# A ViT tower step on one core: mask block sums by TensorE, lo parts by GpSimd, a split first attention and a new prologue order

## The chip, the cores and the metric

One core of a Trainium2 chip runs the whole kernel. The metric is device time in microseconds of one execution, lower is better: 529.68 before, the median of three runs (529.33 to 531.19).

## What is computed

The reference makes a table of time kernels from `log_dt` and `Lambda`, contracts it with `x`, and adds two layers, each behind a layer norm without weights. `mask` is 1024 x 1024 int32; a 32 x 32 block of the attention weight stays if the sum of its mask entries is over zero.

```
P    = dt_Lambda[..., None] * pos - P_max[..., None]
h    = einsum('chn,hnl->chl', Wc, exp(P)).real            # 16 x 128 x 1024
block_mask = mask.reshape(32, 32, 32, 32).sum(axis=(1, 3)) > 0
h    = h + layernorm(h) @ (weight * elem_mask).T
z    = layernorm(h)
h    = h + z @ W_base.T + b_base + sum_e sparsemax(z @ W_router.T + b_router)_e * (z @ A_e) @ B_e
```

## The kernel before

**Tiles and parts.** The 16 x 128 rows of `h` are cut into 16 tiles of 128 rows by 1024 columns. Every large product runs on float32r operands in two parts, hi (the rounded value) and lo (what is left), as three products hi*hi, hi*lo, lo*hi: `product`, L457. One k-chunk of 128 therefore has three matmuls of 512 columns for each of the two column halves, and `attention(t, k)` (L498) and `base(t, k)` (L489) have six. `base` also carries the experts' last product (`experts`, L494).

**The prologue** loads and prepares the weights while the first tiles are made.
- SP's queue loads log_dt, the constants, then by turns eight blocks of 128 rows of the mask and of the attention weight, then x(1), the eight blocks of W_base, lora_A, x(2) and b_router (L324 to L335). Behind them `k_rows(t)` (L316) turns a tile through DRAM into `h1`.
- For weight block j VectorE sums 1024 int32 mask entries to 32 per row (`mask_sums`, L1006), TensorE adds them over 32 rows with one small matmul (`block_sums`, L369), and VectorE masks the weight and takes its row sums (`wa_mask`, L1015). ScalarE centres blocks 0 to 3 (`wa_centre`, L628), GpSimd blocks 4 to 7 (L887). TensorE transposes the block in two halves of four 128 x 128 pieces into the two banks of `acc_b` (`wa_transposes`, L385); ScalarE writes the hi half (`wa_copies`, L634); the lo half is a subtraction from PSUM on VectorE (`wa_lows`, L1023), or, for blocks 1, 3 and 5 (`BY_POOL`), ScalarE copies the bank to SBUF (L637) and GpSimd subtracts there (L892).
- W_base goes the same way without a mask: `wb_half(i)` (L408), `wb_highs` (L643), `wb_lows` (L1029), sixteen halves, two in flight.
- The table of a tile: `phases` and `v_factors` on VectorE, `exponentials` and `sines` on ScalarE, `table_v` on VectorE, `table_b` on GpSimd for tiles 0 to 2 (L876 to L879), and `k_transposed` on TensorE (L439). `k_high` (ScalarE) and `k_low` (VectorE, L1121) make the operands of the attention, `k_turn` (VectorE, L1127) the rows for SP.
- GpSimd's `parameters(r)` (L814) is a chain of 24 small operations; VectorE's `reciprocal_of_norm(r)` (L1001) waits for its tenth link, and GpSimd's end of the chain for that reciprocal.
- The first attention, tile 0, runs in column halves with transpositions in between (`first_attention`, L465, order L546 to L560), the second whole (L566). `attention_residual` (VectorE, L1145) reads all of `acc_a` and gives the row sum for the mean; ScalarE's `h2_centre` and `h2_deviation` follow, and `h2_transposes` (L448), `lora_router` (L479, L481), VectorE's `gates` (L1157 to L1168, which end in `hw_sb`), `gated_transpose` (L487), base and experts. GpSimd's `add_bias` (L917, L920) subtracts the mean and adds b_base; VectorE's `result` (L1187) closes a tile.

**The order** is written out by hand for each engine: TensorE L527 to L591, ScalarE L737 to L802, GpSimd L895 to L912, VectorE L1220 to L1320. Then `steps` runs the loop of all later tiles. Engines wait for each other by semaphores alone, so an instruction that waits holds everything behind it on its engine.

Of the kernel before, what the change touches and what calls it, by code (L numbers as in the profile page):

```python
# [21 lines left out]
P = 128  # L22
# [14 lines left out]
K_ALL = K_COL + 9  # L37
# [6 lines left out]
DT_STEPS = 14  # L44
ROUNDS = (slice(0, 2 * HT), slice(2 * HT, H))
# [3 lines left out]
def constants():  # L49
# [10 lines left out]
        [np.full(NA, NA - 1), np.full(NB0, NA * (NB0 - 1)), np.full(NB1, NA * NB0 * (NB1 - 1))])  # L60
    top = row < N
# [8 lines left out]
def build_vit_tower(nc, x, log_dt, lam, w_attn, mask, w_base, b_base, w_router, b_router, lora_a, lora_b,  # L70
# [4 lines left out]
    with ExitStack() as ctx:  # L75
# [19 lines left out]
        mask_raw, wb_hi = sb_twice("mask_raw", [P, NWT, L], I32, "wb_hi", [P, NWT, KC, P])  # L95
# [31 lines left out]
        x2_hi, x2_lo = sb("x2_hi", [P, KC, P], FR), sb("x2_lo", [P, KC, P], FR)  # L127
        h1 = sb("h1", [P, L])
# [4 lines left out]
        st1, st2 = sb("st1", [P, 8]), sb("st2", [P, 2, 8])  # L133
        gate = sb("gate", [P, 2, E, E])
# [3 lines left out]
        mask_sum = sb("mask_sum", [P, NWT, L // 32])  # L138
# [20 lines left out]
        mask_summed, blk_ready = sem("mask_summed"), sem("blk_ready")  # L159
# [5 lines left out]
        wb_t, wb_high, wb_low = (sem(n) for n in ("wb_t", "wb_high", "wb_low"))  # L165
# [15 lines left out]
        mean_added = sem("mean_added")  # L181
# [17 lines left out]
        def block_bank(j):  # L199

            bank = acc_a[:, HALF:L] if j % 2 else acc_a[:, 0:HALF] if j < NWT // 2 else small
            return bank[:, 0:L // 32]

        BY_POOL = (1, 3, 5)
        CENTRE_LAST = 4
# [99 lines left out]
        def _(sp):  # L307
# [60 lines left out]
        def _(pe):  # L368
            def block_sums(j):  # L369

                pe.wait_ge(mask_summed, j + 1)
                if j >= 2:
                    pe.wait_ge(wa_masked, j - 1)
                pe.matmul(block_bank(j), kst[:, K_BLK:K_BLK + P], mask_sum[:, j, :],
                          start=True, stop=True).then_inc(blk_ready, 1)
# [32 lines left out]
            def wb_half(i):  # L408
                j = i // 2
                if i >= 2:  # L410
                    pe.wait_ge(wb_high, i - 1)
                    pe.wait_ge(wb_low, i - 1)
# [52 lines left out]
            def first_attention(n, chunks, beside=None):  # L465

                for k in chunks:
                    mm = product(acc_a, x2_hi[:, k, :], x2_lo[:, k, :], wa_hi, wa_lo, k, k == 0, k == KC - 1, (n,))
                    if n == 1 and k == KC - 1:  # L470
# [60 lines left out]
            x_transposes(0)  # L531
            block_sums(2)
            wa_transposes(1)
            block_sums(3)
            wa_transposes(2)
            block_sums(4)
            k_transposed(0)
            wa_transposes(3)
            block_sums(5)
            block_sums(6)  # L540
            block_sums(7)
            wa_transposes(4)
            x_transposes(1)
            wa_transposes(5)
            pe.wait_ge(kt_lo, 1)
            wa_rows_ready(NWT // 2)  # L546
            first_attention(0, range(0, 2))
            wa_transposes(6)
            first_attention(0, range(2, 4))
            wa_transposes(7)  # L550
            first_attention(0, range(4, 6))
            pe.wait_ge(rt_in, 16)
            pe.transpose(small[:, HALF - rt_rows:HALF], rt_stage, ident[0:rt_rows, 0:rt_rows]).then_inc(rt_t, 1)
            x_transposes(2)
            wb_half(0)
            wb_half(1)
            first_attention(0, range(6, KC))
            k_transposed(1)
            wa_rows_ready(NWT)
            first_attention(1, range(KC), {0: 2, 2: 3, 3: 4, 4: 5, 6: 6, 7: 7})  # L560
            wb_half(8)

            pe.wait_ge(h2_ready, 1)
            pe.wait_ge(kt_lo, 2)
            half = {1: 9, 2: 10, 3: 11, 4: 12, 5: 13, 6: 14}
            for k in range(KC):  # L566
                attention(1, k)
                if k == KC // 2 - 1:
                    pe.wait_ge(kt_turned, 2)
                    h2_transposes(0, 0)  # L570
                if k in half:
                    wb_half(half[k])
            wb_half(15)
# [5 lines left out]
            for k in range(KC):  # L579
                if k == KC // 2:  # L580
                    k_transposed(2)
                if k == KC - 3:
                    x_transposes(3)
                if k == KC - 2:
                    gated_transpose(0)
                base(0, k)
# [24 lines left out]
        def _(act):  # L611
            def q_tanh(r):
# [26 lines left out]
            def wb_highs(i):  # L639
                act.wait_ge(wb_t, i + 1)  # L640
                if i == 0:
                    act.wait_ge(mask_summed, NWT)
                act.activation(half_of(wb_hi, i), half_bank(i), ACT.Copy).then_inc(wb_high, 1)  # L643

# [30 lines left out]
            def k_high(t):  # L675

                act.wait_ge(kt_ready, t + 1)
                if later(t, 2):
                    act.wait_ge(attn_ready, t)
                act.activation(by_pair(x1_of(t)[0]), kt_pairs, ACT.Copy).then_inc(kt_hi, 1)  # L680

            def h2_centre(t, par):
# [5 lines left out]
                act.activation(h2[par][:, :], h2[par][:, :], ACT.Identity, bias=s[:, 1:2]).then_inc(h2_centred, 1)  # L688

# [54 lines left out]
            act.wait_ge(consts_in, 16)  # L744
            wa_centre(0)
            x_rows_twice(0)
# [3 lines left out]
            sines(0)  # L750
            wa_copies(0)
            sines(1)
            q_sines(1)
            wa_centre(1)
            wa_copies(1)
            wa_centre(2)
            wa_copies(2)
            wa_centre(3)
            x_rows_twice(1)
            q_tanh(1)  # L760
            exponentials(1)
            k_high(0)
            wa_copies(3)
            wa_copies(4)
            wa_copies(5)
            wa_copies(6)
            x_rows_twice(2)
            wa_copies(7)
            wb_highs(0)
            wb_highs(1)  # L770
            k_high(1)
            for i in range(2, 6):
                wb_highs(i)
            k_sum(0)
            k_deviation(0)
            wb_highs(6)
            wb_highs(7)
            act.wait_ge(lora_in, 16 * KC)
            act.wait_ge(rt_copied, 1)
            act.activation(wr[:, :, 0, :], cat_raw, ACT.Copy).then_inc(cat_hi, 1)  # L780
            wb_highs(8)
            exponentials(2)
            h2_centre(0, 0)
            wb_highs(9)
            wb_highs(10)
            sines(2)
            wb_highs(11)
            wb_highs(12)
            h2_high(0)
            for i in range(13, 2 * NWT):  # L790
                wb_highs(i)
            k_sum(1)
            k_deviation(1)
            h2_deviation(0, 0)
            act.wait_ge(lorb_in, 16)
            act.activation(lb_hi[:, :], lb_raw[:, :], ACT.Copy).then_inc(lorb_hi, 1)
            x_rows_twice(3)
            exp_and_sin(3)
            k_high(2)
            gated_high(0)  # L800
            h2_centre(1, 1)
# [4 lines left out]
            act.wait_ge(attn_ready, TILES)  # L806
# [6 lines left out]
        def _(pool):  # L813
            def parameters(r):  # L814
# [79 lines left out]

            parameters(0)  # L895
# [6 lines left out]
            wa_centre(7)  # L902
# [433 lines left out]
```

## Time and profile before

| | |
|---|---|
| median of 3 runs | 529.68 us |
| span of the profiled execution, first to last instruction | 527.4 us |
| time of the profiled execution around its span | not shown |
| TensorE busy | 482.6 us (91% of the span) |
| VectorE, ScalarE, GpSimd busy | 410.9, 256.1, 125.7 us |
| mean granted TensorE clock | 0.982 of full speed |
| VectorE in the first tenth of the span | 70 to 90% or more |
| TensorE from 114.57 us to 500 us | busy 385.43 of 385.43 us |

How to read it: the shares of the whole span say that TensorE bounds the run, but they are an average over two stages. The loop, from 114.57 us on, has TensorE busy all the time. The prologue has it idle or at the lower clock for a good part, and there other engines and the loads set the pace. Matmul ends are modelled, so a busy stretch can hold matmuls at either clock level; the duration of a known piece of work tells which.

### The profile page before, as it was taken

How to read it: one execution, taken by the hardware profiler on the slowest of the kernel's cores; microseconds unless marked ns; L12 is line 12 of the kernel's file. 1: busy time of each engine (PE TensorE's matmuls, PEld its weight loads, DVE VectorE, ACT ScalarE, POOL GpSimd, SP SyncE). 2: the span in 40 equal slices, each digit the busy share in tenths (PEclk: the TensorE clock that was granted, in tenths of full speed). 3: DMA queues.
4: the chain of work that ended last, by engine and by line, in shares of the span. 5: the costliest groups of instructions: out<-in, count | busy, mean ns of one | idle time of the engine just before them, and what ended most of it. 6: DMA issues, size and time to landing. Idle time of an engine off the chain costs nothing.

```text
span 527.4 us, 7434 instructions
## 1 busy us (share of the span) xinstructions
PE 482.6 (91%) x2467; PEld 408.0 (77%) x2467; DVE 410.9 (78%) x866; ACT 256.1 (49%) x469; POOL 125.7 (24%) x110
## 2 busy tenths in 40 slices
PE   2256978979999999999999999999999999999995
PEld 2155757868888888888888888888888888888884
DVE  7989966898888988888888888888878888864241
ACT  3763385956463644546464636363645546223200
POOL 0577952631020303030303020110303030303020
PEclk9996989989999999999999999999999999999999
DMA  8995013022212112120304030212121120303011
GB/s 288 402 312 104 2 41 125 1 57 73 80 47 80 45 48 77 40 85 10 114 0 116 9 93 31 82 42 80 45 70 57 40 81 20 101 15 107 1 40 40
DMA packets 28763, 40.82 MB, mean 77 GB/s; under 512 B 10760, under 2 KB 21192, under 8 KB 28744
## 3 DMA queue, kind: packets, MB, share of 16 engines
q1 hardware_dynamic: 28368, 40.49, 25.3%
q8 instruction: 10, 0.16, 0.1%
q10 hardware_dynamic: 376, 0.10, 0.1%
q14 instruction: 9, 0.07, 0.0%
HBM read 23.80 MB, written 16.78 MB: 77 GB/s over the span
## 4 chain that ended last, share of the span: by engine, by line
PE 86%; DVE 6%; issue 2%; ACT 2%; DMA 1%; POOL 1%; SPq 0%; DVEq 0%; POOLq 0%
PE acc_b L455 36%; PE acc_a L455 33%; PE turnp L439 5%; PE small L479 4%; PE turnp L448 3%; PE small L481 1%; DMA mask_raw<-in_L_attn_mask 1%; PE acc_b L420 1%; DVE wa_raw L1015 1%; PE acc_b L399 1%; DVE mask_sum L1006 1%; PE xps L429 1%; DVE wa_lo L1023 0%; ACT L710 0%; ACT junk L708 0%
## 5 line engine op out<-in xcount | busy, mean ns | idle before, releaser
L917 POOL TENSOR_TENSOR h<-h,st 128x1024 f32<-128x1024 f32 x16 | 30.3, 1895 | 331.0 <-PE turnp L448 331.0
L455 PE MATMUL acc_a<-wa_hi,x_hi 128*128 128x512 f32 x256 | 84.3, 405 | 0.5 <-DVE h L1145 0.5
L455 PE MATMUL acc_b<-wb_hi,x_hi 128*128 128x512 f32 x256 | 84.6, 407 | 0.0
L455 PE MATMUL acc_a<-wa_lo,x_hi 128*128 128x512 f32 x256 | 81.6, 395 | 0.0
L455 PE MATMUL acc_b<-wb_lo,x_hi 128*128 128x512 f32 x256 | 81.3, 394 | 0.0
L455 PE MATMUL acc_a<-wa_hi,x_lo 128*128 128x512 f32 x256 | 81.3, 394 | 0.0
L455 PE MATMUL acc_b<-wb_hi,x_lo 128*128 128x512 f32 x256 | 80.9, 392 | 0.0
L455 PEld LDWEIGHTS acc_a<-wa_hi,x_lo 128*128 128x128 f32 x256 | 48.7, 190 | 10.5
L455 PEld LDWEIGHTS acc_a<-wa_lo,x_hi 128*128 128x128 f32 x256 | 48.9, 191 | 10.2
L455 PEld LDWEIGHTS acc_b<-wb_lo,x_hi 128*128 128x128 f32 x256 | 48.5, 190 | 10.5
L455 PEld LDWEIGHTS acc_b<-wb_hi,x_lo 128*128 128x128 f32 x256 | 48.5, 189 | 10.6
L715 ACT ACTIVATE x_hi<-turnp 128x1024 fp32r<-128x1024 f32 x16 | 16.4, 1025 | 81.0 <-PE turnp L448 81.0
L455 PEld LDWEIGHTS acc_a<-wa_hi,x_hi 128*128 128x128 f32 x256 | 47.1, 191 | 9.1 <-DVE h L1145 0.8
L455 PEld LDWEIGHTS acc_b<-wb_hi,x_hi 128*128 128x128 f32 x256 | 45.0, 190 | 8.2
L1187 DVE SCALAR_TENSOR_TENSOR h<-acc_b,st,h 128x1024 f32<-128x1024 f32 (+1 forms) x17 | 20.7, 1220 | 25.6 <-PE acc_b L455 25.6
L920 POOL TENSOR_TENSOR h<-h,bias 128x1024 f32<-128x1024 f32 x16 | 39.3, 2455 | 1.3
L1121 DVE TENSOR_TENSOR x_lo<-turnp,x_hi 128x1024 fp32r<-128x1024 f32 x16 | 19.6, 1223 | 21.9 <-ACT x_hi L680 21.9
L439 PEld LDWEIGHTS turnp<-v_sb,b_sb 128*128 128x128 f32 x256 | 32.6, 200 | 5.2 <-issue 4.0
L439 PE MATMUL turnp<-v_sb,b_sb 128*128 128x128 f32 x256 | 32.9, 284 | 3.9 <-POOL b_sb L879 3.9
L721 ACT ACTIVATE hw_hi<-small 128x128 fp32r<-128x128 f32 x16 | 4.4, 278 | 60.4 <-PE small L487 60.4
L479 PE MATMUL small<-wr,x_hi 128*128 128x272 f32 x128 | 32.2, 338 | 0.0
L655 ACT ACTIVATE er_t<-er_t 128x256 f32<-128x256 f32 x15 | 6.3, 418 | 49.7 <-DVE er_t L1044 49.7
(201 smaller groups left out, 936.5 us busy)
## 6 DMA issues: line engine op xcount, KB each, us to landing
h<-rows_out SPq DMA_DIRECT2D x16, 512.0 KB, 3.2
out<-h SPq DMA_DIRECT2D x15, 512.0 KB
rows_out<-b_sb SPq DMA_DIRECT2D x56, 128.0 KB, 2.3
mask_raw<-in_L_attn_mask SPq DMA_DIRECT2D x8, 512.0 KB, 9.6
wa_raw<-in_L_attn_weight SPq DMA_DIRECT2D x8, 512.0 KB, 10.2
wb_raw<-in_L_ffn_W_base SPq DMA_DIRECT2D x8, 512.0 KB, 14.9
rows_out<-tmp SPq DMA_DIRECT2D x8, 128.0 KB, 2.3
xn<-in_x SPq DMA_DIRECT2D x15, 64.0 KB
```

The lines of the kernel that those rows point to most:

```text
L399: mm = pe.transpose(half_bank(i)[:, k * P:(k + 1) * P], every_eighth, ident)
L420: mm = pe.transpose(half_bank(i)[:, k * P:(k + 1) * P], wb_rows[j][:, c:c + P], ident)
L439: mm = pe.matmul(kt_pairs[:, h // HG, :, h % HG * C:(h % HG + 1) * C], b_sb[:, h, :, :].rearrange("p x y -> p (x y)"), v_sb[:, h, :, :], s ...
L448: mm = pe.transpose(turnp[:, k * P:(k + 1) * P], h2[par][:, k * P:(k + 1) * P], ident)
L455: return pe.matmul(cols, a, rows, start=first, stop=last)
L479: pe.matmul(small[:, 0:2 * CAT], x_hi[:, k, :], wr[:, k, :, :].rearrange("p s n -> p (s n)"), start=k == 0, stop=False)
L655: act.activation(er_of(t), er_of(t), ACT.Exp).then_inc(tab_exp, 1)
L715: act.activation(x2_of(t)[0][:, :, :].rearrange("p k n -> p (k n)"), turnp[:, :], ACT.Copy)\
L917: pool.tensor_tensor(h2[par][:, :], h2[par][:, :], st2[:, par, 1:2].to_broadcast([P, L]), ALU.subtract)\
L920: pool.tensor_tensor(h2[par][:, :], h2[par][:, :], bias[:, :], ALU.add).then_inc(bias_added, 1)
L1121: dve.tensor_tensor(by_pair(lo), kt_pairs, by_pair(hi).bitcast(F), ALU.subtract).then_inc(kt_lo, 1)
L1187: dve.scalar_tensor_tensor(h, acc_b[:, cols], st2[:, par, 4:5], h, ALU.mult, ALU.add).then_inc(out_ready, 1)
```

## The change

- The mask is turned into numbers in place: blocks 0 to 3 by GpSimd, first in its queue, blocks 4 to 7 by ScalarE. TensorE then sums it over rows with a matrix of ones and zeros (`pick`, placed so that block j adds into rows 4j to 4j + 3), in three groups (0, 1), (2, 3), (4 to 7); VectorE reduces each group's 32 x 1024 sums to 32 x 32; TensorE spreads them over the rows with a second matrix (`spread`, in the place of `h1`).
- Blocks 1 and 4 of W_base get their lo parts from GpSimd: ScalarE copies the transposed bank to SBUF (`wb_copies`), GpSimd subtracts.
- The attentions of tiles 0 and 1 both run by column halves. The first residual is taken by halves too, and the mean is put together from two sums (`first_centre`).
- The last operation of `reciprocal_deviation` is a tensor_scalar in place of a tensor_tensor. SP's `k_rows(0)` waits for all block sums, GpSimd's first `add_bias` for `hw_ready`.
- The order of the prologue is another one on all four engines. The loop of the later tiles is not touched beyond that one operation and the count of `attn_ready`, which starts with tile 1.

The diff's core:

```diff
+MASK_GROUPS = ((0, 1), (2, 3), (4, 5, 6, 7))
+    k[:, K_PICK:K_PICK + PICK] = np.arange(PICK)[None, :] == L // 32 - 4 + row[:, None] // 32
...
+        WB_BY_POOL = (1, 4)
...
             def k_rows(t):
                 sp.wait_ge(kt_turned, t + 1)
+                if at(t, 0):
+                    sp.wait_ge(blk_ready, NWT)
...
-            def block_sums(j):
-                pe.wait_ge(mask_summed, j + 1)
-                if j >= 2:
-                    pe.wait_ge(wa_masked, j - 1)
-                pe.matmul(block_bank(j), kst[:, K_BLK:K_BLK + P], mask_sum[:, j, :],
-                          start=True, stop=True).then_inc(blk_ready, 1)
+            def mask_by_rows(j):
+                g = GROUP_OF[j]
+                first, last = j == MASK_GROUPS[g][0], j == MASK_GROUPS[g][-1]
+                if j == 0:
+                    pe.wait_ge(pick_ready, 1)
+                if g >= 2 and first:
+                    pe.wait_ge(mask_summed, g - 1)
+                pe.wait_ge(mask_cast[j], 1)
+                for n in range(2):
+                    mm = pe.matmul(rows_bank(g)[:, n * HALF:(n + 1) * HALF], pick[:, MB - 4 - 4 * j:2 * MB - 4 - 4 * j],
+                                   mask_num[:, j, n * HALF:(n + 1) * HALF], start=first, stop=last)
+                if last:
+                    mm.then_inc(mask_rowed, 1)
+            def block_sums(g):
+                if g == 0:
+                    pe.wait_ge(spread_ready, 1)
+                    pe.wait_ge(turn_step, 3)
+                else:
+                    pe.wait_ge(wa_masked, MASK_GROUPS[g][0])
+                pe.wait_ge(mask_summed, g + 1)
+                for j in MASK_GROUPS[g]:
+                    mm = pe.matmul(block_bank(j), spread[:, j * P:(j + 1) * P], mask_sum[:, g, :], start=True, stop=True)
+                mm.then_inc(blk_ready, len(MASK_GROUPS[g]))
...
+            mask_by_rows(0)
             dt_transposes()
+            mask_by_rows(1)
+            mask_by_rows(2)
+            mask_by_rows(3)
             block_sums(0)
             block_sums(1)
+            x_transposes(0)
             wa_transposes(0)
+            mask_by_rows(4)
+            mask_by_rows(5)
+            mask_by_rows(6)
+            mask_by_rows(7)
+            wa_transposes(1)
+            wa_transposes(2)
             block_sums(2)
             k_transposed(0)
             wa_transposes(3)
+            x_transposes(1)
             wa_transposes(4)
...
             wa_transposes(5)
+            wa_transposes(6)
+            wa_transposes(7)
...
+            attention_half(0, 0, (4,))
             wb_half(0)
             wb_half(1)
+            attention_half(0, 0, (5,))
...
+            wb_half(2)
+            wb_half(3)
             k_transposed(1)
+            wb_half(4)
+            wb_half(5)
...
+            pe.wait_ge(h2_half, 1)
+            pe.wait_ge(kt_lo, 2)
+            attention_half(1, 0, (0,))
...
+            pe.wait_ge(kt_turned, 2)
+            h2_transposes(0, 0)
...
+            pe.wait_ge(h2_ready, 1)
+            attention_half(1, 1, (0,))
...
             lora_router(0)
+            wb_half(14)
+            wb_half(15)
+            k_transposed(2)
             pe.wait_ge(wb_high, 2 * NWT)
-            pe.wait_ge(wb_low, 2 * NWT)
+            pe.wait_ge(wb_low, len(wb_direct))
+            pe.wait_ge(wb_low_pool, len(WB_BY_POOL))
...
+            def mask_numbers(j):
+                act.wait_ge(mask_in[j], 16)
+                act.activation(mask_num[:, j, :], mask_rows[j], ACT.Copy).then_inc(mask_cast[j], 1)
...
+            def wb_copies(i):
+                act.wait_ge(wb_t, i // 2 * 2 + 2)
+                act.activation(wb_raw[:, i // 2, i % 2 * HALF:(i % 2 + 1) * HALF], half_bank(i), ACT.Copy)\
+                    .then_inc(wb_copied, 1)
...
+            def first_centre():
+                s = st2[:, 0, :]
+                act.wait_ge(h2_half, 1)
+                act.activation(half_mean[:, 0:1], s[:, 0:1], ACT.Copy, scale=-1.0 / L).then_inc(h2_mean_half, 1)
+                act.wait_ge(h2_ready, 1)
...
+            mask_numbers(4)
+            x_rows_twice(0)
+            wa_centre(0)
+            wa_centre(1)
+            mask_numbers(5)
+            mask_numbers(6)
+            sines(1)
+            mask_numbers(7)
             wa_copies(0)
...
+            wb_highs(3)
+            wb_copies(2)
+            wb_copies(3)
+            k_high(1)
+            exponentials(2)
...
+            sines(2)
+            first_centre()
+            wb_highs(6)
+            h2_deviation(0, 0)
...
+            mask_numbers(0)
+            mask_numbers(1)
+            mask_numbers(2)
+            mask_numbers(3)
             parameters(0)
             table_b(0)
...
             table_b(2)
+            wb_lows(1)
+            wb_lows(4)
             pool.wait_ge(lorb_hi, 1)
...
             pool.wait_ge(bias_in, 16)
+            pool.wait_ge(hw_ready, 1)
             add_bias(0, 0)
...
-            def mask_sums(j):
-                dve.wait_ge(mask_in[j], 16)
-                dve.tensor_reduce(mask_sum[:, j, :], mask_rows[j].rearrange("p (k b) -> p k b", b=32), AX.X, ALU.add)\
+            def mask_sums(g):
+                dve.wait_ge(mask_rowed, g + 1)
+                dve.tensor_reduce(mask_sum[:, g, :], rows_bank(g).rearrange("p (k b) -> p k b", b=32), AX.X, ALU.add)\
                     .then_inc(mask_summed, 1)
...
-                dve.tensor_tensor(s[:, 4:5], s[:, 5:6], s[:, 7:8], ALU.mult).then_inc(s_chain, 1)
+                dve.tensor_scalar(s[:, 4:5], s[:, 5:6], s[:, 7:8], None, ALU.mult).then_inc(s_chain, 1)
```

VectorE's order up to the first result is now: dt_exponential, signs, dec_and_turn, phases(0), mask_sums(0), q_arguments(0) and (1), reciprocal_of_tanh(0), mask_sums(1), wa_mask(0) and (1), reciprocal_of_norm(0), decay_b(0), phases(1), v_factors(0), wa_mask(2) and (3), wa_lows(0), mask_sums(2), table_v(0), wa_mask(4), wa_lows(2), wa_mask(5) to (7), wa_lows(4), decay_b(1), k_low(0), k_turn(0), the router's copy, wa_lows(6), v_factors(1), wa_lows(7), reciprocal_of_tanh(1), wb_lows(0) and (1), table_v(1), phases(2), k_low(1), h1_reciprocal(0), first_residual(0) and (1), reciprocal_of_norm(1), k_turn(1), wb_lows(4) and (5), decay_b(2), v_factors(2), phases(3), wb_lows(6) and (7), table_v(2), wb_lows(10) and (11), h2_low(0), wb_lows(12) to (15), h2_reciprocal(0), gates(0), h1_reciprocal(1), attention_residual(1), gated_low(0), k_low(2), k_turn(2), v_factors(3), table_v(3), result(0).

## Rows read from the trace of the kernel before

**Rows 1.** Windows: us, busy time and instructions by engine, clock, DMA, GB/s

```profile
0.00:48.57 48.57, 18.78 (x87) 17.05 (x87) 42.41 (x96) 24.89 (x52) 23.18 (x43) 0.92 0.87 289
48.57:114.57 66.00, 56.86 (x295) 45.89 (x294) 52.25 (x98) 43.61 (x77) 37.29 (x37) 0.93 0.13 43
114.57:500.00 385.43, 385.43 (x1988) 327.38 (x1987) 308.47 (x651) 186.09 (x338) 60.98 (x28) 1.00 0.21 59
```

**Rows 2.** Timeline of TensorE, 46 to 110: start, length, instruction, [idle before, releaser]

```profile
46.97 1.95 PE L399 MATMUL acc_b<-kst,wa_raw 128*128 128x128 f32 x8 [3.16 <-DVE wa_lo L1023]
...
53.82 1.28 PE L399 MATMUL acc_b<-kst,wa_raw 128*128 128x128 f32 x8
...
65.32 0.63 PE L420 MATMUL acc_b<-kst,wb_raw 128*128 128x128 f32 x4 [0.55 <-ACT wb_hi L643]
...
71.09 0.63 PE L420 MATMUL acc_b<-kst,wb_raw 128*128 128x128 f32 x4 [1.49 <-issue]
73.53 0.63 PE L420 MATMUL acc_b<-kst,wb_raw 128*128 128x128 f32 x4 [1.81 <-ACT wb_hi L643]
...
90.90 0.63 PE L420 MATMUL acc_b<-kst,wb_raw 128*128 128x128 f32 x4 [0.97 <-issue]
...
108.71 0.33 PE L487 MATMUL small<-kst,hw_sb 128*128 128x128 f32 x1 [3.19 <-DVE hw_sb L1168]
```

**Rows 3.** Chain of waits, 55 to 133: start, length, engine, tile, line, count

```profile
55.10 1.40 PE acc_a L455 x6
...
74.69 4.61 PE acc_a L455 x12
...
82.94 0.87 PE turnp L448 x8
...
85.65 0.44 PE acc_b L420 x4
...
109.04 5.69 PE acc_b L455 x18
...
115.60 10.93 PE acc_a L455 x48
126.53 1.79 PE turnp L439 x16
...
130.17 2.82 PE acc_b L455 x12
```

**Rows 4.** Timeline of VectorE: columns as in rows 2

```profile
38.57 1.23 DVE L1015 SCALAR_TENSOR_TENSOR wa_raw<-acc_a,wa_raw 128x1024 f32<-128x1024 f32 x1 [2.24 <-PE acc_a L374]
...
46.13 0.09 DVE L1015 DVE_READ_ACCUMULATOR wa_raw<-acc_a,wa_raw 128x1 f32 x1
...
56.45 1.81 DVE L995 TENSOR_SCALAR lb_raw<-bias 128x224 f32<-128x224 f32 x1
...
101.13 1.79 DVE L1139 TENSOR_TENSOR st<-st 128x1 f32<-128x1 f32 x1
```

**Rows 5.** Groups by line and shape, 0 to 115: busy, mean ns, idle before

```profile
L1006 DVE TENSOR_REDUCE mask_sum<-mask_raw 128x32 f32<-128x1024 int32 x8 | 9.6, 1212 | 0.2
...
L892 POOL TENSOR_TENSOR wa_lo<-wa_raw,wa_hi 128x1024 fp32r<-128x1024 f32 x3 | 7.1, 2378 | 0.0
...
L1023 DVE TENSOR_TENSOR wa_lo<-acc_b,wa_hi 128x512 fp32r<-128x512 f32 x10 | 6.4, 682 | 1.0 <-ACT wa_hi L634 1.0
...
L887 POOL TENSOR_SCALAR wa_raw<-wa_raw,wa_neg 128x1024 f32<-128x1024 f32 x4 | 4.5, 1120 | 0.4
L1127 DVE STREAM_TRANSPOSE tmp<-turnp 128x1024 f32<-128x1024 f32 x2 | 4.1, 2072 | 0.0
```

**Rows 6.** Tile view of mask_raw, window 5.4:5.8 (block 3, issued at 5.44)

```profile
DMA to landing us min/median/max: 9.1/9.1/9.1
```

**Rows 7.** Timeline of GpSimd: columns as in rows 2

```profile
55.73 2.39 POOL L892 TENSOR_TENSOR wa_lo<-wa_raw,wa_hi 128x1024 fp32r<-128x1024 f32 x1
...
100.54 2.37 POOL L912 TENSOR_TENSOR lb_lo<-lb_raw,lb_hi 128x1024 fp32r<-128x1024 f32 x1 [3.94 <-ACT lb_hi L796]
```

More of the change, by code:

```diff
@@ L127, in build_vit_tower @@
         x2_hi, x2_lo = sb("x2_hi", [P, KC, P], FR), sb("x2_lo", [P, KC, P], FR)
+        with nc.sbuf_tensor("spread", [L // 32, L], F) as spread:
+            pass
         h1 = sb("h1", [P, L])
@@ L199, in block_bank, with rows_bank @@
         def block_bank(j):
[L201 to L202 removed]
+            return small[:, j * MB:(j + 1) * MB]
+        def rows_bank(g):
+            return (turnp if g == 1 else acc_a)[0:MB, :]
         BY_POOL = (1, 3, 5)
+        WB_BY_POOL = (1, 4)
+        wb_direct = [i for i in range(2 * NWT) if i // 2 not in WB_BY_POOL]
+        wb_raws = [i for i in range(2 * NWT) if i // 2 in WB_BY_POOL]
         CENTRE_LAST = 4
@@ L544, in _ @@
             wa_transposes(5)
+            wa_transposes(6)
+            wa_transposes(7)
+            pe.wait_ge(mask_summed, len(MASK_GROUPS))
             pe.wait_ge(kt_lo, 1)
             wa_rows_ready(NWT // 2)
[L547 to L553, printed above, removed]
@@ L564, in _ @@
[L564 to L573, printed above, removed]
+            attention_half(0, 0, (5,))
+            attention_half(0, 0, (6,))
+            attention_half(0, 0, (7,))
@@ L574, in _ @@
+            wb_half(13)
             pe.wait_ge(h2t_lo, 1)
@@ L576, in _ @@
             lora_router(0)
+            wb_half(14)
+            wb_half(15)
+            k_transposed(2)
             pe.wait_ge(wb_high, 2 * NWT)
-            pe.wait_ge(wb_low, 2 * NWT)
[L579 to L586, printed above, removed]
+            pe.wait_ge(wb_low, len(wb_direct))
+            pe.wait_ge(wb_low_pool, len(WB_BY_POOL))
+            base(0, 0)
+            base(0, 1)
+            base(0, 2)
+            base(0, 3)
+            gated_transpose(0)
+            base(0, 4)
+            base(0, 5)
+            base(0, 6)
+            base(0, 7)
             pe.wait_ge(lorb_lo, 1)
@@ L1253, in _ @@
             decay_b(1)
-            v_factors(1)
-            table_v(1)
-            wa_lows(6)
-            wa_lows(7)
-            reciprocal_of_tanh(1)
+            k_low(0)
+            k_turn(0)
             dve.wait_ge(rt_t, 1)
@@ L1262, in _ @@
                             small[:, HALF - rt_rows:HALF].rearrange("p (e k) -> p k e", e=E)).then_inc(rt_copied, 1)
+            wa_lows(6)
+            v_factors(1)
+            wa_lows(7)
+            reciprocal_of_tanh(1)
             wb_lows(0)
             wb_lows(1)
+            table_v(1)
             phases(2)
-            for i in range(2, 5):
-                wb_lows(i)
             k_low(1)
+            h1_reciprocal(0)
+            first_residual(0)
+            dve.wait_ge(b_ready, 2)
+            first_residual(1)
+            reciprocal_of_norm(1)
             k_turn(1)
+            wb_lows(4)
             wb_lows(5)
-            h1_reciprocal(0)
-            wb_lows(6)
-            dve.wait_ge(b_ready, 2)
-            attention_residual(0, 0)
-            wb_lows(7)
-            wb_lows(8)
-            reciprocal_of_norm(1)
-            wb_lows(9)
-            wb_lows(10)
             decay_b(2)
             v_factors(2)
+            phases(3)
+            wb_lows(6)
+            wb_lows(7)
+            table_v(2)
+            wb_lows(10)
             wb_lows(11)
-            phases(3)
+            h2_low(0)
             wb_lows(12)
-            h2_low(0)
             wb_lows(13)
```

207 lines of the change are left out of this document (130 added, 77 removed).

## The prediction

> **What bounds the kernel now.** The stages by windows come first [rows 1]. From 114.57 us on TensorE is busy without a gap at the full granted clock, and the loop that runs there has the same instructions in the same order after the change. So I price only how early TensorE reaches that point, the end of the first FFN's experts. Between 48.57, the first attention matmul, and 114.57 it is busy 56.9 of 66.0 us, part of that at the low level.
>
> The TensorE timeline says where it stood [rows 2]: 0.55 and 1.81 for a ScalarE copy of a wb half, 1.49 before a wb half, 0.97 before another, 3.19 for `hw_sb`: 8.0 us in five places. The chain of waits shows what follows a long wait [rows 3]: 48 attention matmuls take 10.93, so 12 should take 2.73 and 18 should take 4.10; after the waits at 74.69 and 109.04 they took 4.61 and 5.69. Clock thus cost 1.9 and 1.6.
>
> The same view prices the work: an attention 10.93, k_transposed 1.79, h2_transposes 0.87, a wb half 0.44, lora_router 130.17 - 128.32 = 1.85; base has 48 matmuls like an attention, experts six, 1.37. Two attentions, base, experts, sixteen wb halves, two k_transposed, one h2_transposes and one router make 47.5 us. At 55.10 all wa rows were transposed and four half chunks done (2.8 by the 1.40 of two), so a TensorE that never waits would have ended at 55.10 + 44.7 = 99.8. It ended at 114.57: 14.8 lost, of which 8.0 + 3.5 are named; 3.3 are short waits and small transposes, which I carry over whole.
>
> **Start: when the last wa rows are transposed.** Before, wa_transposes(7) ran at 53.82 [rows 2], and the masks that feed it were the end of VectorE's queue: wa_mask(7) ended at 46.2 [rows 4]. VectorE was full up to there, so its queue is the sum. Removed: eight mask reductions, 8 x 1.14 net of overlap (1.21 each) = 9.1, and k_low(0) and k_turn(0), now behind the masks, 1.2 (a pass, as a reduction) + 2.0 with overlap = 3.2 [rows 5]. Added: three reductions over 32 partitions, same length per partition, 3.6. Gone: the wait of 2.2 at 38.57 [rows 4].
>
> New waits: (a) dt_transposes stands on TensorE behind block 0's two matmuls; these wait for a GpSimd conversion. A 128x1024 one-input pass on GpSimd takes 1.12 and one with two inputs 2.38 [rows 5]; no row shows the int32 one. I take 1.12, the same inputs and shape, and keep 2.38. VectorE needs dt_transposes next, so it stands where it used to reduce block 0: 1.12 and 0.9 in front of them, 2.1 with the hand-over. (b) Block 3 lands 9.1 after its issue, at 14.5 [rows 6]; plus 1.12 and two matmuls of 512 columns (0.45 each, an estimate above the mean of 4.61 / 12 in a stretch partly at the low level) it is at 16.5, where VectorE would come at 15.6: 0.9 of waiting. (c) GpSimd starts `parameters(0)` behind four conversions, about 1.5 later, and VectorE's reciprocal_of_norm(0) with everything queued behind it waits that long. (d) wa_mask(4) waits for block_sums(2), which TensorE has behind wa_transposes(2): 0.8. (e) two-input VectorE work beside the conversions is held, below: 1.3. Sum 46.2 - 9.1 - 3.2 + 3.6 - 2.2 + 2.1 + 0.9 + 1.5 + 0.8 + 1.3 = 41.9.
>
> From there VectorE has two lo pairs, 1.25 each with overlap (0.68 a half) [rows 5], a decay (0.8, an estimate from pass lengths), k_low 1.2 and k_turn 2.1 before wa_transposes(7) is free: 41.9 + 6.6 = 48.5. It begins when the first half pair is done, 47.9, and eight cold transposes take 1.95 [rows 2]; I take 50.4 as its end. Ends: 48.5 with no holds, 55 with a 2.38 conversion and every hold.
>
> **What is held.** L1139, a two-input operation of one element per partition, took 1.79 from 101.13 and ended at 102.92, with the GpSimd subtraction that ran from 100.54 to 102.91 [rows 4, 7]. So two-input VectorE work waits for the GpSimd instruction in flight. Its replacement by a tensor_scalar stays off the path now. New on the path is table_v(2)'s last addition: both inputs in SBUF, and by my order it meets table_b(2) on GpSimd; 1.6, ends 0 and 2.4. [...]
>
> **Then TensorE's queue from 50.4.** 47.5 of work and 3.3 carried make 101.2. The first twelve matmuls come after scattered work and pay 1.9 [rows 3]. The big wait, for attention_residual(0), goes: column half 0 of attention(0) is read by first_residual(0) while half 1 runs. By my count TensorE wants it at about 68 and VectorE has it at 67.4, behind table_v(1), phases(2), k_low(1) and the reciprocals: cover half a us, and each us past it costs one. What is late next is h2_transposes(0), which needs both residuals and ScalarE's centring behind sines(2): 0.8, ends 0 and 4. The wait for `hw_sb` goes: h2_deviation(0) moves ahead in ScalarE's queue, and add_bias(0) waits for hw_ready, so the gates are not held; VectorE ends them at about 93, TensorE asks at 96. Behind that new wait GpSimd has only later biases, and result(0) stands behind table_v(3) on VectorE anyway.
>
> Four wb lo halves go to GpSimd: two passes of 2.38 plus four ScalarE copies in place of four VectorE ones of 0.68; GpSimd is otherwise free after table_b(2) and is done at about 88, base asks at 91. The wait put into SP's first k_rows holds k_rows(1), lora_B, bias and x loads, but its eight block sums are out by 37 and the turn it waits for anyway comes at 47. The four ScalarE conversions stand between loads; their end is in (d). The selectors, the sixteen mask matmuls and the block sums cost nothing by themselves: up to 48.57 TensorE is busy 18.8 us and ScalarE 24.9 [rows 1]. Were that cover gone, the matmuls would add 16 x 0.45 = 7.2.
>
> End 101.2 + 1.9 + 0.8 + 1.6 = 105.5 against 114.57: 9.1 saved. The profiled span is 527.4, so 518.3; what lies around a span is not shown, the median of the runs is 2.3 above it, so **520.5**.
>
> **Rivals.** [...] 0.12. *The wait is only moved*: VectorE or ScalarE brings the first residual or its centring as late as before, TensorE again stands about 4 and pays the clock 1.9, 5.5 beyond my 0.8: 526.0. For it: a cover of half a us. Against: the split, and VectorE has four lo halves, 2.7 us, less. 0.11. Both together: 529.2, no change, 0.06. *Slower: conversion on GpSimd*. If int32 to float costs far more there than any pass in the trace, four of them in a row set mask block 3: 5.4 + 4c in place of 15.6. The saving is gone at c = 4.8, and at c = 7 the kernel takes 538. For it: no integer row on GpSimd, which the kernel now starts with. Against: its 128x1024 passes lie between 1.1 and 2.5. 0.06.
>
> **How the numbers follow.** 0.65 for the forecast, whose own range is 514.5 (no holds, no cold start, no centring wait, 5.6 less, with 0.4 at the start) to 523. The range goes on to 526.5 for the first two rivals, 8 in 10. A change of 0.5%, 2.6 us, is about what can be told from none: faster 0.65 + 0.12 + 0.11 = 0.88, same 0.06, slower 0.06.
>
> **What would show it.** In the changed profile: conversions on GpSimd near 1.1 each; the last wa_mask ended by 42 and the last wa transposition by 50.4; no wait over 1 us of TensorE between the attentions; no wait for `hw_sb`; TensorE busy without gap from about 105 on, and the loop as long as before. Wrong would be conversions over 2.6, an hw_sb wait, or a wait of several us for the first residual.

## The result, and the profile after

The changed kernel takes 527.87 us, the median of ten runs (523.77 to 528.86), beside 530.68 for the kernel before in ten runs (529.20 to 531.58): a ratio of 0.9944, 95% interval 0.9922 to 0.9965. That is 2.8 us faster, where 9.1 were forecast, and 1.4 us above the upper end of the forecast range, 526.5. The profiled execution took 528.11, its span 526.3.

First the windows of the changed kernel, columns as in rows 1: up to the first attention matmul, and the window of the loop that rows 1 has for the kernel before.

```profile
0.00:52.88 52.88, 28.76 (x119) 21.35 (x120) 40.89 (x97) 32.79 (x64) 29.63 (x48) 0.83 0.79 263
...
114.57:500.00 385.43, 385.43 (x1953) 321.56 (x1952) 299.34 (x639) 181.64 (x329) 57.16 (x27) 1.00 0.20 56
```

Then its chain of waits, columns as in rows 3. L440 is a wa transposition, L499 a 512-column matmul, L492 h2_transposes.

```profile
46.90 1.17 ACT wa_hi L734 x2
48.07 0.50 ACT wa_raw L737
48.70 1.73 PE acc_b L440 x8
50.45 0.70 DVE wa_lo L1168
51.29 1.94 PE acc_b L440 x8
53.23 4.77 PE acc_a L499 x15
...
105.69 0.87 PE turnp L492 x8
106.56 11.20 PE acc_a L499 x48
...
121.40 2.84 PE acc_b L499 x12
...
135.24 11.20 PE acc_a L499 x48
```

Read it from the middle. h2_transposes(1), with which the loop begins, starts at 105.69; in the chain of before it starts 0.87 ahead of the attention at 115.60 [rows 3], at 114.73. The prologue is 9.04 us shorter. From there to the end of the span it takes 526.3 - 105.69 = 420.6, and before 527.4 - 114.73 = 412.7. **The loop is 7.9 us longer**, and that is where the gain went. 9.04 less 7.9 is the 1.1 by which the two spans differ; the medians differ by 2.8, as single executions of either kernel spread by more than 2.

It is longer without a wait and at the same granted clock: from 114.57 to 500 TensorE is busy 385.43 of 385.43 us at 1.00 in both, with 1953 matmuls on record instead of 1988 [rows 1]. What differs is the pace of the 512-column matmuls: 48 of them take 11.20, 233.3 ns each, where they took 10.93, 227.7 [rows 3]; 12 take 2.84, where they took 2.82. Transpositions keep their 0.87 [rows 3]. A tile goes from 106.56 to 135.24, 28.68 us, and in the chain of before from 115.60 [rows 3] to 143.77, 28.17:

```profile
143.77 10.92 PE acc_a L455 x48
```

### The profile page after: what moved, and what is told of

It is laid out like the page before. It is cut to its first block, busy times and chain, and to the rows that moved or that the text cites. A ratio compares the mean times of both kernels' runs of the same rounds, so it can differ in the third digit from the quotient of the medians.

```text
span 526.3 us, 7475 instructions
## 1 busy us (share of the span) xinstructions
PE 495.0 (94%) x2483; PEld 409.4 (78%) x2483; DVE 400.8 (76%) x859; ACT 261.9 (50%) x480; POOL 135.6 (26%) x116
## 4 chain that ended last, share of the span: by engine, by line
PE 90%; ACT 3%; DVE 3%; POOL 1%; issue 1%; DMA 1%; SPq 0%; DVEq 0%; ACTq 0%
PE acc_b L499 38%; PE acc_a L499 33%; PE turnp L483 6%; PE small L525 4%; PE turnp L492 3%; PE acc_b L440 2%; PE small L527 2%; PE acc_b L464 1%; DMA mask_raw<-in_L_attn_mask 1%; ACT wa_hi L734 1%; PE xps L473 1%; DVE wa_raw L1160 0%; PE small L415 0%; PE small L533 0%; ACT wa_raw L737 0%
## 5 line engine op out<-in xcount | busy, mean ns | idle before, releaser
L499 PE MATMUL acc_a<-wa_hi,x_hi 128*128 128x512 f32 x256 | 85.5, 405 | 0.0
L499 PE MATMUL acc_b<-wb_hi,x_hi 128*128 128x512 f32 x256 | 84.8, 407 | 0.0
L499 PE MATMUL acc_a<-wa_hi,x_lo 128*128 128x512 f32 x256 | 83.5, 397 | 0.0
L499 PE MATMUL acc_a<-wa_lo,x_hi 128*128 128x512 f32 x256 | 83.5, 397 | 0.0
L499 PE MATMUL acc_b<-wb_lo,x_hi 128*128 128x512 f32 x256 | 81.8, 396 | 0.0
L499 PE MATMUL acc_b<-wb_hi,x_lo 128*128 128x512 f32 x256 | 81.7, 395 | 0.0
L499 PEld LDWEIGHTS acc_a<-wa_hi,x_lo 128*128 128x128 f32 x256 | 48.4, 189 | 11.7
L499 PEld LDWEIGHTS acc_a<-wa_lo,x_hi 128*128 128x128 f32 x256 | 48.5, 190 | 11.4
L499 PEld LDWEIGHTS acc_b<-wb_hi,x_lo 128*128 128x128 f32 x256 | 48.1, 188 | 11.7
L499 PEld LDWEIGHTS acc_b<-wb_lo,x_hi 128*128 128x128 f32 x256 | 48.1, 188 | 11.4
L499 PEld LDWEIGHTS acc_a<-wa_hi,x_hi 128*128 128x128 f32 x256 | 47.5, 190 | 10.2
L499 PEld LDWEIGHTS acc_b<-wb_hi,x_hi 128*128 128x128 f32 x256 | 44.8, 189 | 9.1
L1272 DVE STREAM_TRANSPOSE b_sb<-turnp 128x1024 f32<-128x1024 f32 x14 | 31.3, 2239 | 0.0
```

The lines of the kernel that those rows point to most:

```text
L499: return pe.matmul(cols, a, rows, start=first, stop=last)
L1272: dve.transpose(turned_of(t).rearrange("p (g x a) -> p g a x", g=G, a=NA), kt_pairs).then_inc(kt_turned, 1)
```

## Experiments

TensorE's instructions in the loop are the same.
### The place of the tiles, moved in both kernels

Edits: to the changed kernel 32 bytes behind `kst` (e1), or in front of `x1_hi` (e3); to the kernel before 224 bytes behind `kst` (e2); e4 is the changed kernel once more.

```diff
         kst = sb("kst", [P, K_ALL])
+        sb("pad", [P, 8])
```

> The changed kernel with 32 unused bytes per partition behind the constants, so that every tile behind them begins at a multiple of 64 bytes again, as before the change; nothing else differs. Theory A (the loop got longer by where the operands of the products lie in SBUF): 48 attention matmuls of the loop take 10.92 again in place of 11.20, a tile's period 28.13 in place of 28.66, the span is 8 us shorter, about 518.3, and the time near 520. Rival B (the pace of the loop belongs to the execution: a fuller prologue, the chip or the activity): 11.20 stays, and the time stays at 527 to 528.

> The kernel before with 224 unused bytes per partition behind the constants, so that every tile behind them lies where the change puts it; order and instructions are those of before. Theory A: 48 attention matmuls of the loop take 11.20, the prologue's end stays near 114.6, and the time is 8 us longer, 537 to 539. Rival B: 10.92 stays and the time stays at 529 to 531.

> The changed kernel with the 32 unused bytes only in front of the hi and lo parts of h (x1_hi and all tiles behind it begin at a multiple of 64 bytes, the tables, v_sb and b_sb do not). If it is the operands of attention and base that count (theory A in its narrow form): 48 attention matmuls take 10.92 and the span is about 518 to 519. If tiles in front of them count as well: between 10.92 and 11.20. Rival B: 11.20 and a span of 526.

> The changed kernel once more, as it is. Theory A: 48 attention matmuls take 11.20 again and the prologue ends near 105.5, in every execution. Rival B in the form that the pace changes from one execution to the next: anything between 10.9 and 11.2.

The kernel after with 32 bytes took 519.48 (six runs, 517.85 to 522.48), a ratio to the kernel before of 0.9797 (0.9769 to 0.9824); the kernel before with 224 bytes took 538.74 (four runs), 1.0163 (1.0139 to 1.0187). e3 took 519.43 in one execution, e4 527.21. Chain of waits of e1:

```profile
106.28 0.87 PE turnp L493 x8
...
128.94 5.47 PE acc_b L500 x24
...
135.28 10.92 PE acc_a L500 x48
```

and of e2:

```profile
116.34 0.87 PE turnp L449 x8
...
145.87 11.21 PE acc_a L456 x48
```

Each kernel takes the other's pace with its place. The loops are 519.0 - 106.28 = 412.7 for e1 and 536.9 - 116.34 = 420.6 for e2; e3 gives 412.6, e4 420.5. So it is shown that the 7.9 us are a matter of placement and not of the prologue's new order, and e3 puts it on the x tiles or on what lies behind them.

### Which tiles, and which rule

Edits: e5 puts x1 and x2 where e1 has them and everything behind them 128 bytes beyond where the change had it, so that it stays off; e6 puts everything behind `kst` at 64 modulo 128; e7, on e1, moves `wa_hi`, a moving operand, by 32 bytes, and everything behind it, x1 and x2 too, by 128.

```diff
+        sb("pad", [P, 8])
         x1_hi = sb("x1_hi", [P, KC, P], FR)
...
         x2_hi, x2_lo = sb("x2_hi", [P, KC, P], FR), sb("x2_lo", [P, KC, P], FR)
+        sb("pad2", [P, 24])
```

> The kernel after, with 32 bytes in front of x1_hi and 96 bytes behind x2_lo: x1 and x2 (hi and lo) begin at multiples of 128 bytes again (193920 and on), and every tile behind them stays where the changed kernel had it, at 32 modulo 64. Theory (the stationary x tiles alone count): 48 attention matmuls take 10.9, and the time from the start of h2_transposes(1) to the end of the span is 412.7 plus at most 0.6, since the experts' stationary hw_hi and hw_lo stay off (6 of the 102 matmuls of 512 columns in a tile, 16 tiles, 6 ns each). Rival (a tile behind them counts, h1, h2 or hw): 11.2 and 420.5.

> The kernel after, with 96 bytes behind kst: x1_hi begins at 193984, which is 64 modulo 128. Theory (a start at a multiple of 64 is enough): 48 attention matmuls in 10.9, the loop 412.7. Rival (it must be a multiple of 128): 11.2 and 420.5, as with 96 modulo 128.

> The kernel after with the 32 bytes behind kst, and wa_hi alone, the moving operand of 32 of the 48 attention matmuls, 32 bytes off (114848, 32 modulo 64); everything else at the place modulo 128 that it had. Theory (only the stationary operand counts): 48 matmuls in 10.9, the loop 412.7. Rival (either operand counts): 10.92 + 32 x 0.006 = 11.11, and the loop 16 x 0.19 = 3.0 longer, 415.7.

They took 521.14, 529.38 and 527.87, one execution each. Chain of waits of e5 (the x24 are base and, at its end, the experts' six):

```profile
105.17 0.87 PE turnp L494 x8
...
127.88 5.55 PE acc_b L501 x24
...
134.31 10.93 PE acc_a L501 x48
```

of e6:

```profile
106.91 0.87 PE turnp L493 x8
...
136.47 11.20 PE acc_a L500 x48
```

and of e7:

```profile
106.33 0.88 PE turnp L495 x8
...
129.38 5.57 PE acc_b L502 x24
...
135.82 11.18 PE acc_a L502 x48
```

e5 says that the attention's pace is that of the x tiles: 10.93, with every tile behind them still off. Its loop is 1.4 longer than e1's, where at most 0.6 was expected: the group with the experts' six, whose stationary tiles stayed off, takes 5.55 against 5.47 in e1. e6 is slow, 420.7: a start at a multiple of 64 is not enough. e7 overturned the theory: with x at 0 modulo 256 the attention is slow, and so is the base product, whose own operands stayed at multiples of 128. Its 48 matmuls take 11.18, not the rival's 11.11, so "either operand's 32 bytes" does not fit either. What fits the attention and the base product in all of them is the distance: x1_hi lies a multiple of 256 bytes behind wa_hi in the kernel before, e1, e3 and e5, and 224, 224, 64 and 96 off in after, e2, e6 and e7; x2_hi lay 128 off wb_hi in e7.

### The distance of the two operands

Edits, both on e1: e12 moves all tiles by 32 bytes, so that the distances stay; e13 moves x1 and x2 alone by 128.

```diff
+        sb("pad2", [P, 8])
         wa_raw, wa_lo = sb_twice("wa_raw", [P, NWT, L], F, "wa_lo", [P, NWT, KC, P])
```

> The kernel after with the 32 bytes behind kst, and 32 bytes in front of the first tile, so that every tile, stationary or moving, begins 32 bytes further on and the distances between them stay (x1_hi 193952, wa_hi 114848, wa_lo 16544). Theory now (the distance between the stationary and the moving operand counts, and must be a multiple of 256 bytes; it fits the slow base product of the run with wa_hi moved, where x2 stood 128 off, and the slow run with x 64 off): 48 attention matmuls in 10.9, the loop 412.7. Rival (each operand's own address modulo 256 counts, 128 being the fast one): 11.2 and 420.5.

> The kernel after with the 32 bytes behind kst, and x1 and x2 (hi and lo) alone 128 bytes further on (194048); the tiles behind them 256 further. Theory (the distance must be a multiple of 256): 48 attention matmuls in 11.2, the loop 16 x 0.49 longer at 420, the experts' six matmuls alone at the old pace. Rival (a multiple of 128 is enough, and the run with wa_hi moved was slow from wa_hi's 32 bytes alone): 10.9 and 412.7.

They took 519.95 and 526.02, one execution each. Chain of waits of e12:

```profile
105.42 0.87 PE turnp L494 x8
...
134.43 10.92 PE acc_a L501 x48
```

and of e13:

```profile
104.52 0.87 PE turnp L495 x8
...
127.57 5.58 PE acc_b L502 x24
...
134.03 11.15 PE acc_a L502 x48
```

| run | x1_hi starts at | wa_hi starts at | distance modulo 256 | 48 matmuls | loop |
|---|---|---|---|---|---|
| before | 193664 | 114816 | 0 | 10.93 | 412.7 |
| after, e4, e2 | 193888 | 114816 | 224 | 11.19 to 11.21 | 420.5 to 420.6 |
| e1, e3 | 193920 | 114816 | 0 | 10.90 to 10.92 | 412.6 to 412.7 |
| e5 | 193920 | 114816 | 0 | 10.93 | 414.1 |
| e6 | 193984 | 114816 | 64 | 11.20 | 420.7 |
| e7 | 194048 | 114848 | 96 (128 to wa_lo) | 11.18 | 419.8 |
| e12 | 193952 | 114848 | 0 | 10.92 | 412.7 |
| e13 | 194048 | 114816 | 128 | 11.15 | 419.7 |

(Starts are bytes within a partition, in the compiled program.) In e12 wa, wb and x start 32 bytes off a multiple of 64, and the loop is as fast as before. In e13 they all start at multiples of 128, and it is slow. So in the attention and the base product the distance fits every run, and of those tried only multiples of 256 bytes are fast.

Two things keep this from being a rule. The experts' six matmuls do not follow it: in e13 their `hw` and `lb` lie a multiple of 256 bytes apart, at the places modulo 256 that they have in e1, and the old pace was expected of them, but base and experts together take 5.58, against 5.47 in e1. Read one by one from the traces, the experts' matmuls start 231 to 232 ns apart in e13, and in e7 too, where the distance is also a multiple of 256 (70 steps each); it is 226.6 in e1 and 233.4 in the changed kernel. Whether the pace of the base matmuls just before carries over or something else counts is open. And the distance is not separated from the start of x alone: x1 starts at 128 or 160 modulo 256 in all fast runs, at 0, 96 or 192 in all slow ones. A run with x at 160 and wa at 128 would tell, and there is none. Which matmul's moving operand it is, the one that streams while the next weights are loaded (weight loads are busy 321.56 of the 385.43 us of the changed kernel's window above, in which the matmuls leave no gap) or the matmul's own, these runs can't tell, since hi and lo of a weight lie a multiple of 256 apart (but for e7). Why it costs 5.8 ns a matmul stays open too.

### What the prologue's parts carry

All on e1. e8 and e14 take the first residual half only when both column halves are done, as the unsplit one did; e15 is e1 once more.

```diff
-                dve.wait_ge(attn_half, n + 1)
+                dve.wait_ge(attn_half, 2)
```

> The kernel after with the 32 bytes behind kst, and first_residual(0) waiting for both column halves of attention(0). From the end of wa_transposes(7) to the start of h2_transposes(1) the two profiles with the x tiles at 64 bytes took 51.9 and 52.0. Theory (the split hides one residual half, and what is lost is that half): TensorE waits about 1.0 (0.75 and the hand-over) for h2_half in front of attention(1), the centring comes 0.8 later too, and the stretch takes 53 to 53.5. Rival (the split is what kept the wait of several us and the clock away): 55 or more, with attention(1) at a lower granted clock.

> The kernel with first_residual(0) waiting for both column halves of attention(0) once more, timed in rounds beside the split one. Its single look, 516.3, had a higher granted clock in the wa transpositions (0.78 against 0.59 to 0.70 from 30 to 50), and from wa_transposes(7) on took 51.6 against 51.9. Theory (the early start was chance, the split hides only what ScalarE's queue in front of the centring would have hidden): median within 1 us of the split kernel's 519.5. Rival (the whole residual is better in itself): 516 to 517. Rival (the split is worth its half): 520.5 to 521.5.

> The kernel after with the 32 bytes behind kst once more, for comparison on the same chip: 519.5, as before, and 517.9 to 522.5 in single executions. If the granted clock of the start is what spreads them, a profile with a higher clock from 30 to 50 ends the prologue earlier by as much.

e8 took 516.29 in one execution; in four each, e14 took 519.57 (517.25 to 521.15, ratio 0.9788, 0.9746 to 0.9831) and e15 519.86 (519.53 to 521.40, ratio 0.9805, 0.9775 to 0.9835). **The split is worth nothing that can be told.** TensorE's waits from 52 to 106 in e14 (columns: what waited, for what, us in total, times, longest):

```profile
PE acc_a L500 <- DVE h L1300: 0.9, 1, 0.9
PE acc_b L465 <- issue: 0.2, 1, 0.2
```

and in e15, with the split:

```profile
PE turnp L493 <- ACT h L806: 1.1, 1, 1.1
```

Without the split TensorE waits 0.9 for the residual, and then no longer waits for the centring: the same wait, one step earlier. The wait of several us that the rival foresaw isn't there in either. e8's lead was made before: TensorE's timeline has, in e8,

```profile
29.89 1.28 PE L441 MATMUL acc_b<-kst,wa_raw 128*128 128x128 f32 x8 [0.71 <-DVE wa_lo L1169]
```

and in e1

```profile
30.39 1.94 PE L441 MATMUL acc_b<-kst,wa_raw 128*128 128x128 f32 x8 [0.59 <-DVE wa_lo L1169]
```

This is the same work at the high and at the low level: the granted clock is 1.00 in the 1.28 us and 0.50 in the 1.94. From 30 to 50 us it is 0.78 in e8 and 0.59 in e1. The last wa transposition then ends at 50.20 in e8, at 54.29 in e1. In e15 the clock of that stretch is 0.71, the end 53.01.

e9 gives the lo parts of wb blocks 1 and 4 back to VectorE, in the places of its queue where they stood before relative to `k_low(1)` and `table_v(2)`, and takes ScalarE's copies out.

```diff
-        WB_BY_POOL = (1, 4)
+        WB_BY_POOL = ()
...
+            wb_lows(2)
+            wb_lows(3)
             k_low(1)
...
+            wb_lows(8)
+            wb_lows(9)
             table_v(2)
```

> The kernel after with the 32 bytes behind kst, and the lo parts of wb blocks 1 and 4 by VectorE again, in front of k_low(1) and of table_v(2), without ScalarE's four copies. Theory (VectorE's queue feeds the first residual and the base product): two lo halves, 1.36, stand in front of the first residual, which had about 1 us in hand, and four in front of the base product, where GpSimd's two passes set the start before; the stretch from wa_transposes(7) to h2_transposes(1) takes 52.5 to 54.5. Rival (the move to GpSimd paid nothing, as its passes of 4.7 us ended just before the base product began): 51.0 to 52.

It took 524.09, 4.6 above e1. From wa_transposes(7) to h2_transposes(1) it takes 109.61 - 52.56 = 57.05, where e15 takes 52.00: 5.05 more, beyond either expectation. Its TensorE waits from 52 to 110:

```profile
PE acc_b L465 <- issue: 2.5, 2, 2.1
PE xps L474 <- DVE v_sb L1234: 1.4, 1, 1.4
PE small L526 <- DVE x_lo L1322: 0.5, 1, 0.5
```

and its chain of waits behind the first of them:

```profile
64.81 2.06 issue
66.87 1.45 PE acc_b L465 x8
68.32 2.56 PE acc_a L500 x6
```

VectorE comes to the lo halves 2 and 3 only behind table_v(1) and phases(2), at 66.09; TensorE waits 2.06 for them in front of the next wb halves, and then runs at a granted clock of 0.61 from 66.87 to 70.88: eight transpositions 1.45 instead of the 0.87 of e14, six matmuls 2.56 instead of 1.38, 1.8 more. GpSimd's share is thus the largest single part of the prologue's gain that was taken alone. The size belongs to the new order: in e9 table_v(1) and phases(2) stand between lo halves 1 and 2, in the kernel before only phases(2).

e10 centres the first tile ahead of sines(2); e11 converts mask block 0 once more on GpSimd, ahead of the others.

```diff
+            first_centre()
             sines(2)
-            first_centre()
```

> The kernel after with the 32 bytes behind kst, and on ScalarE first_centre ahead of sines(2). Theory (h2_transposes(0) is late only because of sines(2), 2.4 us in front of the centring): TensorE's wait in front of h2_transposes(0) goes, 1.0, and the stretch from wa_transposes(7) to h2_transposes(1) takes 51.0. Rival (VectorE's table_v(2) and the wb halves behind it are what is late next, as sines(2) comes 1.6 later): 52 or more.

```diff
+            pool.wait_ge(mask_in[0], 16)
+            pool.tensor_copy(h2[1][:, :], mask_rows[0])
             mask_numbers(0)
```

> The kernel after with the 32 bytes behind kst, and one more conversion of mask block 0 on GpSimd, in front of the others, into h2_1, where nothing reads it: about 1.04 more in front of the first mask matmul. Theory of the prediction (the conversion, dt_transposes behind it and VectorE behind these are one chain): the last wa_mask ends 0.5 to 1.5 later than 43.3, and the loop starts as much later. Rival (ScalarE's wa halves set the end of the wa transpositions, with VectorE in hand): wa_mask later, but wa_transposes(7) ends within 0.5 of the 53.1 to 54.3 it had.

e10 took 519.16, within what single executions of e1 spread. From wa_transposes(7) on it takes 51.9 (52.74 to 104.62): e1's value, close to the rival's 52 and not the theory's 51.0. The wait for the centring went and another came, its TensorE waits being

```profile
PE acc_b L465 <- issue: 1.4, 1, 1.4
```

in front of a pair of wb halves at 80.58. e11 took 520.90; the last wa_mask ended at 43.5, 0.2 behind e1's, the last wa transposition at 54.5 (54.3), the loop began at 106.42 (106.28). The theory of one chain got less than its 0.5. VectorE's `dec`, behind dt_transposes, starts 1.8 later than in e1 (9.88, 8.07), its wa_mask(0) only 0.3 (19.21, 18.95): what stands between took it up. The rival's condition, an end of the wa transpositions within 0.5, holds.

## Why the prediction was wrong, point by point

**The step that failed is the premise**: "the loop that runs there has the same instructions in the same order after the change. So I price only how early TensorE reaches that point". The instructions are the same; their operands are not in the same place. The diff showed `K_ALL` growing and `kst` standing in front of the x tiles, but no row of one kernel can show what a place costs, and I gave the loop no term. It took 7.9 of the 9.04 us. "The loop as long as before" was named as a sign, and it was the one that told. With the x tiles put back (e1, e15) the kernel takes 519.5 to 519.9, where 520.5 was forecast.

**The prologue's sum came out, partly by chance.** It was to end at 105.5, and ended at 105.69. It has two halves: the last wa transposition was to end at 50.4 and ended at 53.23; the rest was to take 55.1 and took 52.46: 2.8 late and 2.6 early. Before the change the last wa transposition ended at 55.10 [rows 2], so 1.87 of the 9.04 came ahead of it and 7.17 behind. No run puts the mask sums alone back on VectorE; what they are worth by themselves is not shown.

The start, first on VectorE's timeline of after:

```profile
8.62 0.35 DVE L1119 TENSOR_SCALAR dec<-small,lam_sb 128x128 f32<-128x128 f32 x1 [2.65 <-PE small L423]
...
9.26 0.95 DVE L1122 TENSOR_SCALAR turn<-turn 128x128 f32<-128x128 f32 x1
...
11.83 1.07 DVE L1194 SCALAR_TENSOR_TENSOR gh_t<-u_t,kst 128x192 f32<-128x192 f32 x1
...
14.42 0.81 DVE L1129 TENSOR_SCALAR lb_raw<-dec,flip 128x16 f32<-128x16 f32 x1
...
22.91 0.25 DVE L1146 RECIPROCAL lb_raw<-lb_raw 128x16 f32<-128x16 f32 x1 [1.52 <-POOL lb_raw L991]
...
37.49 1.23 DVE L1160 SCALAR_TENSOR_TENSOR wa_raw<-small,wa_raw 128x1024 f32<-128x1024 f32 x1 [1.93 <-PE small L415]
...
42.12 1.22 DVE L1160 SCALAR_TENSOR_TENSOR wa_raw<-small,wa_raw 128x1024 f32<-128x1024 f32 x1
...
84.14 1.29 DVE L1240 TENSOR_TENSOR v_sb<-tmp,v_sb 128x1024 f32<-128x1024 f32 x1
```

and on GpSimd's:

```profile
5.94 1.04 POOL L946 CAST mask_num<-mask_raw 128x1024 fp32r<-128x1024 int32 x1 [5.51 <-DMA mask_raw<-in_L_attn_mask]
9.10 1.04 POOL L946 CAST mask_num<-mask_raw 128x1024 fp32r<-128x1024 int32 x1 [2.13 <-DMA mask_raw<-in_L_attn_mask]
...
57.05 2.39 POOL L1013 TENSOR_TENSOR b_sb<-b_sb,h 128x1024 f32<-128x1024 f32 x1
...
84.42 3.26 POOL L1013 TENSOR_TENSOR b_sb<-b_sb,h 128x1024 f32<-128x1024 f32 x1
87.65 4.71 POOL L1031 TENSOR_TENSOR wb_lo<-wb_raw,wb_hi 128x1024 fp32r<-128x1024 f32 x2
```

- *Conversion*: 1.04 measured, 1.12 taken; the rival of the slow conversion is out.
- *The new waits of VectorE*: (a) 2.65 for dt_transposes, 2.1 taken; (b) none for mask block 3, 0.9 taken; (c) 1.52 for `parameters(0)`, 1.5 taken; (d) 1.93 for block_sums(2), 0.8 taken; (e) beside a conversion L1122 took 0.95, and 0.23 in e1, where none ran beside it; two more were held alike (L1194 1.07, L1129 0.81, against 0.44 and 0.22 for such operations with no conversion beside them): together 1.9, 1.3 taken. Together 1.4 over the sum, and the last wa_mask ended at 43.34 instead of 41.9. The three started while a conversion ran and ended at 10.21, 12.90 and 15.23, the conversions at 10.14, 12.70 and 15.21; L1122 and L1129 are TENSOR_SCALARs, so it was not work on two tensors alone that was held. Nor was all such work: a wa_mask (L1160) took 1.22 from 28.31 beside GpSimd's L1010, which ran from 27.40 to 29.33, and 1.21 from 20.18 beside none of GpSimd's long operations. The 0.12 among the rivals is for holds of 4.5 at the start (4 x 1.12), an estimate that no run shows; 1.9 came.
- *From there to 53.23*: I let VectorE's queue set the end. The chain shows ScalarE's halves and copies (46.90 to 48.57) and transpositions wholly or mostly at the low level (1.94 at a granted clock of 0.50, 1.73 at 0.61) taking turns, 9.9 us where I had 8.5. This term was mis-sized for want of the engine that came last.

The rest, 52.46 us:

- *Cold clock*: 15 matmuls took 4.77 from 53.23, at a granted clock of 0.72, 1.27 over 15 x 0.2333; 1.9 taken.
- *h2_transposes(0)* waited 1.03 for the centring; 0.8 taken. By e10 it is worth nothing to remove: the wb halves are late next.
- *table_v(2)'s last addition* took 1.29, hardly held; 1.6 taken. GpSimd was the later one: the addition started at 84.14, L1013 at 84.42, and L1013 took 3.26 instead of 2.39. My order of the two was wrong.
- *hw_sb*: no wait, as forecast. *GpSimd's lo parts* were done at 92.36, not 88, just ahead of the base product's start at 92.89; the cover of three us was half a us.
- *Short waits* carried over: 3.3 taken; 52.46 - 47.5 - 1.27 - 1.03 - 0.07 leaves 2.6, and 0.9 of that is the slower pace (150 matmuls by 5.8 ns, an estimate). TensorE's waits from 50 to 106 in after are few:

```profile
PE turnp L492 <- ACT h L805: 1.0, 1, 1.0
PE acc_b L440 <- DVE wa_lo L1168: 0.9, 1, 0.9
PE acc_b L464 <- issue: 0.2, 1, 0.2
```

The mechanism that I named for the big wait, the split of the residual, is not what removed it: e14 does without the split and loses nothing. What did more is a line that I costed only as an aside, four lo halves off VectorE: e9 puts them back and loses 5.05, in one execution and in the new order.

## What to carry to other kernels

A change to one tile's size moves all tiles behind it, and a loop whose code is untouched changed pace by it here (48 matmuls from 10.93 to 11.20): compare the duration of a known group of matmuls in the two profiles before any part of the change is judged. In this kernel the 32 bytes of padding that put x a multiple of 256 bytes from wa and wb again are worth 1.5% (0.9797 against 0.9944 of the kernel before). The 7.9 us of the loop, lost without a wait and at a granted clock of 1.00 in both, were a matter of pace, and padding in both kernels (e1, e2) told that it was placement.

## What the runs showed of the hardware

- The attention's 512-column float32r matmuls, each with a weight load of its own (2483 of each on the page of the changed kernel), started every 227 to 228 ns in the kernel before, e1, e3, e5 and e12, where x1_hi lies a multiple of 256 bytes from wa_hi, and every 232 to 234 ns at a distance modulo 256 of 224 (the changed kernel, e2, e4), 64 (e6), 96 (e7) or 128 (e13) (10.90 to 10.93 against 11.15 to 11.21 for 48). The experts' six, at 231 to 232 ns in e7 and e13 with a multiple of 256, show that the distance is not the whole of it. What causes it no run shows.
- The level at which TensorE runs the first wa transpositions varies between executions: eight took 1.28 us in e8 and 1.94 in e1, at a granted clock of 1.00 and 0.50, with 0.78 and 0.59 from 30 to 50 us, and single executions of e1 spread from 517.85 to 522.48.
